# Wide-head attention: values of both examples in one product, weighted values turned by the product itself

## The chip, the cores and the metric

The kernel runs on one core of a Trainium2 chip, as one program. The metric is the device time of one execution in microseconds (us), smaller is better. The engines that matter here are TensorE (PE, matrix products and transposes), VectorE (DVE), ScalarE (ACT) and GpSimd (POOL); each works through its own queue in order, and they wait for each other by semaphores. TensorE reads from SBUF and writes into PSUM, which has eight banks of 512 floats for each of 128 partitions. A product has a stationary operand, loaded first (LDWEIGHTS, shown as PEld), and a moving operand that streams through. All products in this part are in float32, and the profile shows each of them as two MATMUL records; a transpose is one.

## The reference

The whole kernel is a stack of four layers (cross attention, then a feed-forward part) on 32 examples of 64 tokens, 128 wide. The change is in the second layer's attention: 16 heads of 64, queries from the doubly normalised tokens `x`, keys and values from the context, a softmax over 64 context rows for each head, and a gated residual. In short:

```
x1 = layernorm(x);  xn = layernorm(x1) * gamma + beta
q = xn @ w_q;  k, v = split(context @ w_kv)            # 16 heads of 64
p = softmax(q k^T / 8, over the 64 context rows of the example)
x = x + tanh(gate) * ((p v) @ w_out + b_out)
```

## The kernel before, in words

`wide_head_attention` works on 16 tiles. A tile is 128 tokens, two examples of 64, which the code calls b = 0 and 1. The 16 heads are held as eight pairs c, with u = 0 and 1 for the even and the odd head. The work is written as a pipeline of steps by hand (`step(n, p)` for each engine): step n computes the keys of tile n, the queries of tile n-1, the scores and the values of tile n-2, transposes the probabilities and weighs the values of tile n-3, and projects the output of tile n-4. The order of the calls in `step` is the order of each engine's queue, and nothing else sets it. Steps 7 to 14 run in a loop of two steps, the others are unrolled.

TensorE's parts in a step of before, with the lines under which the profile shows them: `scores` (L967, 32 products of 64x64x64, into `pS`), `turn_x` (L941, one transpose), `turn_probs` (L978, eight transposes of `prob` into `pP`), `queries` (L953, eight products of 128x128x128), `turn_out` (L1004, eight transposes of `on` into `pP`), `keys` (L916, as `queries`), `weigh_values` (L993, 32 products of 64x64x64, into `pO`), `project` (L1011, eight products of 128x128x128 that add up in one place of `pP`) and `values` (L931, four products of 128 rows by 64 columns by 512: for each example b and each u).

Queries, keys and values share the two PSUM banks J0 and J1. Each user waits until ScalarE or VectorE has copied out what the user before left there. ScalarE copies `xnT` (L1047), `probT` (L1055), `qT` (L1063), `oT` (L1071) and `kT` (L1079) to SBUF and takes the exponential of `prob` (L1084). VectorE does the two layer norms (L154, L139, L142, L144), the maximum and its subtraction from the scores (L1121, L1123), the sum and its reciprocal (L1133, L1135), the scaling of the weighted values by it (L1140, `on`), the bias and the residual (L1146, L1148) and the copies of the values (L1161). GpSimd copies the context tile (L1094) and takes the powers for the norms (L150).

## Time and profile before

| | us |
|---|---|
| median of 3 runs (1015.64 to 1017.59) | 1017.44 |
| the profiled execution, its own time | 1015.85 |
| its span in the trace | 1014.1 |
| TensorE busy | 787.3 |
| VectorE busy | 625.4 |
| ScalarE busy | 468.8 |
| first product of this attention | 151.4 |
| its last bias add (L1146) | 347.3 |

Times inside the trace count from the start of the span. The profile names an instruction by its engine, its line in the kernel, what it writes and what it reads. "Busy" is the time in which at least one instruction of the engine was in flight; a MATMUL record lasts longer than its share of the array, because successive ones overlap, so the distance from start to start is what a group costs. "issue" is a wait that the profile can't put down to another engine. Names of several buffers are shortened, so `A_v`, `A_on` and `L1w` are tiles of this attention (`L1w` holds its weights).

### The profile page before, as it was taken

What the parts mean: (1) busy time and instruction counts of PE and PEld (TensorE: products, weight loads), DVE (VectorE), ACT (ScalarE), POOL (GpSimd) and SP (SyncE); (2) the same over time, 40 slices, a digit from 0 to 9 for tenths busy, and PEclk for the clock granted to TensorE, in tenths of its full rate; (3) what the DMA queues carried; (4) which work ended last, traced back from release to release, by engine and by line L of the source; (5) the groups of instructions that cost most, each with busy time, mean ns of one, the idle gap of its engine ahead of it and who ended that gap; (6) DMA issues with size and microseconds to landing.
All of it is one profiled execution on the core that took longest, in us unless ns stands there. A gap on an engine that the chain in (4) does not pass through costs nothing.

```text
span 1014.1 us, 24106 instructions
## 1 busy us (share of the span) xinstructions
PE 787.3 (78%) x8041; PEld 650.9 (64%) x8041; DVE 625.4 (62%) x1617; ACT 468.8 (46%) x928; POOL 369.0 (36%) x482
## 2 busy tenths in 40 slices
PE   6998889999999689997377775568777569969005
PEld 3766787888887579996267764467777526643005
DVE  3886766777777677776453333652222388867795
ACT  3886425455544344442144433034454327735753
POOL 5663602111110261101466663125566545550810
PEclk9999699999999979999599999568999769978557
DMA  6300000000000000033323214101111300000001
GB/s 186 96 0 1 1 1 2 3 2 1 0 0 3 1 5 22 21 104 89 103 83 99 72 42 107 41 17 37 43 42 42 90 20 2 0 1 1 0 0 41
DMA packets 49218, 36.06 MB, mean 36 GB/s; under 512 B 7665, under 2 KB 44978, under 8 KB 49138
## 3 DMA queue, kind: packets, MB, share of 16 engines
q1 hardware_dynamic: 43420, 24.45, 8.5%
q0 software_dynamic: 4992, 10.23, 3.7%
q8 instruction: 48, 0.79, 0.3%
q10 hardware_dynamic: 726, 0.33, 0.1%
q14 instruction: 32, 0.26, 0.1%
HBM read 26.73 MB, written 8.26 MB: 35 GB/s over the span
## 4 chain that ended last, share of the span: by engine, by line
PE 67%; DVE 14%; issue 6%; ACT 4%; another core or an unknown queue 3%; DMA 2%; DVEq 2%; POOL 2%; ACTq 1%; SPq 0%; POOLq 0%
PE psum L2057 9%; PE psum L1413 7%; PE psum L2082 4%; PE psum L1011 3%; PE psum L916 3%; PE psum L953 3%; PE psum L931 3%; PE psum L2354 2%; PE psum L308 2%; PE psum L1382 2%; PE psum L1383 2%; PE psum L1384 2%; PE psum L993 2%; PE psum L648 2%
## 5 line engine op out<-in xcount | busy, mean ns | idle before, releaser
L2057 PE MATMUL psum<-E_XT,E_weights 128*128 128x128 f32 x780 | 115.0, 300 | 45.1 <-DVE E_XT L2206 19.1
L2057 PEld LDWEIGHTS psum<-E_XT,E_weights 128*128 128x128 f32 x780 | 103.6, 210 | 54.0 <-DVE E_XT L2206 23.2
L2178 POOL DMA_INDIRECT y_scratch<-E_y,route_place_of x78 | 78.5, 1006 | 74.6 <-DVE E_y L2231 32.0
L2170 POOL DMA_INDIRECT E_rows<-rows_scratch,route_token_of x78 | 77.2, 990 | 58.2 <-DVE route_token_of L1887 29.9
L1670 DVE SCALAR_TENSOR_TENSOR X<-psum,E_gates,X 128x128 f32<-128x128 f32 x256 | 71.8, 345 | 26.2 <-PE psum L1413 25.8
L1413 PEld LDWEIGHTS psum<-E_w,E_h 128*128 128x128 f32 x512 | 67.8, 194 | 11.5 <-ACT E_h L1499 6.0
L2137 ACT ACTIVATE E_h<-psum,cols 128x128 f32<-128x128 f32 x156 | 44.6, 369 | 65.5 <-issue 30.7
L1499 ACT ACTIVATE E_h<-psum,cols 128x512 f32<-128x512 f32 x64 | 43.9, 690 | 61.4 <-PE psum L1384 61.3
L1413 PE MATMUL psum<-E_w,E_h 128*128 128x128 f32 x512 | 68.6, 277 | 4.7 <-ACT E_h L1499 4.0
L2221 DVE TENSOR_TENSOR E_h<-E_sg,psum 128x384 f32<-128x384 f32 x39 | 21.6, 554 | 68.4 <-PE psum L2057 32.0
L203 POOL TENSOR_TENSOR rstd<-vareps,nhalf 128x4 f32<-128x4 f32 x24 | 24.7, 1030 | 104.2 <-DVE vareps L197 104.2
L220 PE MATMUL psum<-ident,xn 128*128 128x128 f32 x80 | 20.2, 402 | 43.0 <-DVE xn L211 33.6
L220 PEld LDWEIGHTS psum<-ident,xn 128*128 128x128 f32 x80 | 13.7, 209 | 50.3 <-issue 25.2
L2082 PE MATMUL psum<-L1w,E_h 128*128 x312 | 43.5, 284 | 0.5 <-DVE E_y L2233 0.5
L150 POOL TENSOR_TENSOR A_A_inner_rstd<-A_A_inner_vareps,nhalf 128x1 f32<-128x1 f32 x16 | 8.8, 551 | 96.0 <-DVE A_A_inner_vareps L144 96.0
L2343 PE MATMUL psum<-ident,Q_amax_rows 128*1 128x128 f32 x5 | 1.8, 352 | 52.4 <-DVE Q_amax_rows L2451 51.7
L2233 DVE TENSOR_TENSOR E_y<-psum,E2b2all 128x128 f32<-128x128 f32 x39 | 11.4, 291 | 50.3 <-PE psum L2082 29.3
L773 POOL TENSOR_TENSOR A_kexp<-E_first,hmask 128x512 f32<-128x512 f32 x32 | 32.7, 1043 | 25.7 <-PE psum L648 25.6
L2082 PEld LDWEIGHTS psum<-L1w,E_h 128*128 128x128 f32 x312 | 39.6, 199 | 1.0 <-issue 0.7
L2053 PE MATMUL psum<-ident,E_rows 128*128 128x128 f32 x78 | 22.8, 292 | 22.3 <-DMA E_rows<-rows_scratch,route_token_of 22.3
L2120 ACT ACTIVATE E_weights<-E_first 128x768 f32 x39 | 33.0, 845 | 14.1 <-issue 13.8
L1047 ACT ACTIVATE A_xnT<-psum,cols 128x128 f32<-128x128 f32 x16 | 7.3, 458 | 64.3 <-PE psum L941 64.3
(342 smaller groups left out, 2164.0 us busy)
## 6 DMA issues: line engine op xcount, KB each, us to landing
routed_back<-y_scratch SPq DMA_DIRECT2D x16, 256.0 KB, 4.8
E_first<-in_L_xattn_W SPq DMA_DIRECT2D x1, 2048.0 KB, 8.6
L1w<-in_L_xattn_W SPq DMA_DIRECT2D x8, 256.0 KB, 4.5
rows_scratch<-xn SPq DMA_DIRECT2D x8, 256.0 KB, 2.3
E_w<-in_L_ffn_routed_w SPq DMA_DIRECT2D x28, 64.0 KB, 1.8
E_raw<-in_L_ffn_w_down SPq DMA_DIRECT2D x8, 176.0 KB
E_rows<-rows_scratch,route_token_of POOLq DMA_INDIRECT x78
y_scratch<-E_y,route_place_of POOLq DMA_INDIRECT x78
```

The source lines that it names most:

```text
L220: tr = pe.transpose(self.bank[:, i * P:(i + 1) * P], self.m.xn[:, g * GT + i, :], self.m.ident[:, :])
L773: ke = pool.tensor_tensor(kexp[:, p, b], kk.broadcast_to([P, HP, S]), m.hmask[:, :].rearrange("p (h o) -> p h o", o=1).broadcast_to([P, HP ...
L916: mm = pe.matmul((J1, J0)[j][:, c * P:(c + 1) * P], w["k"][:, cc * P:(cc + 1) * P], columns(m.ctxT, t, P), start=True, stop=True)
L1413: mm = pe.matmul(y_bank(e, g)[:, i * P:(i + 1) * P], h[:, g % 2, c, i * P:(i + 1) * P], w2[:, p, c, :], start=(c == 0 and i == 0), stop=(c ...
L1499: act.activation(h[:, g % 2, c, :], ring[(C * g + c) % 4], spec["func"], bias=spec["b1"][:, bass.ds(e * C + c, 1)]).then_inc(h_ready.sem, 1)
L1670: st = dve.scalar_tensor_tensor(out=m.X[:, t, :], in0=y_bank(e, g)[:, i * P:(i + 1) * P], scalar=gates[:, t, bass.ds(e, 1)], in1=m.X[:, t, :],
L2057: mm = pe.matmul(out[:, c * P:(c + 1) * P], WE[:, p, (k0 + c) * P:(k0 + c + 1) * P], XT[:, p, :], start=True, stop=True)
L2082: mm = pe.matmul(Y[p][:, 0:P], h[:, p, c, :], W2[:, bass.ds(e, 1), c, :].rearrange("p o d -> p (o d)"), start=c == 0, stop=c == C - 1)
L2120: act.activation(WE[:, i % 2, :], W1[:, bass.ds(e, 1), :].rearrange("p o f -> p (o f)"), ACT.Copy).then_inc(w_ready.sem, 1)
L2137: ac = act.activation(h[:, p, c, :], m.banks[2 + i % 3][:, c * P:(c + 1) * P], spec["func"], bias=spec["b1"][:, bass.ds(e * C + c, 1)])
L2170: pool.indirect_dma_start(out=xg[:, i % 4, :], out_offset=None, in_=rows[:, :], in_offset=bass.IndirectOffsetOnAxis(ap=disp.token_of[:, i: ...
L2178: pool.indirect_dma_start(out=yrows[:, :], in_=y[:, i % 3, :], in_offset=None, out_offset=bass.IndirectOffsetOnAxis(ap=disp.place_of[:, i: ...
```

## The change

The values of a tile are now two products of 128 context rows (both examples) by 128 by 512, one for the even heads into J1, one for the odd heads into J0. VectorE copies the even heads into partitions 0 to 63 of `v`, ScalarE the odd heads into partitions 64 to 127, each in two copies of 64 partitions by 512.

`weigh_values` swaps its operands, so that the result comes out with head dimension by token and needs no transpose: the eight transposes of `turn_out` and the tile `on` are gone. In PSUM, example b now fills bank b of `pO`, and the half of the partitions for head parity u is `x = (u + b) % 2`. So for example 1 the two halves of each pair of heads are swapped; `project` therefore takes a second copy of the output weights with its halves swapped (`L1wo_halves_changed`, two more loads of 256 KB each), and becomes 16 products with 64 columns of the stationary operand instead of eight with 128. The division by the sum of the exponentials, which was in `on`, is now done on `prob` in place, before `turn_probs`, with one VectorE instruction of 128x1024.

The order in a step changes too. On TensorE `project` comes third and `weigh_values` last; on ScalarE the copy of `oT` comes first, straight from `pO`, and the copy of the odd heads' values stands before the exponential; on VectorE the sum, the reciprocal, the scaling of `prob` and the residual come first. Blocks that only moved are left out here.

```diff
-        on = sb("on", [P, 2, H * dh])
-        oT = sb("oT", [P, 2, HP, P])
+        oT = sb("oT", [P, 2, 2, HP, S])
...
-    ov = pO.rearrange("p u (c d) -> p u c d", d=dh)
+    ov = pO.rearrange("p b (c q) -> p b c q", q=S)
...
         def values(t, p):
             pe.wait_ge(*ctx1_ready(t + 1))
             wv = w["v"].rearrange("p (c u d) -> p c u d", u=2, d=dh)
-            for b in range(2):
+            for u in range(2):
                 if before_end(t, 2):
-                    pe.wait_ge(*k_ready(2 * t + b + 5))
+                    pe.wait_ge(*k_ready(2 * t + u + 5))
...
-                for u in range(2):
-                    mm = pe.matmul((J1, J0)[b][u * S:(u + 1) * S, :], ctx1[:, p, b * S:(b + 1) * S], wv[:, :, u, :],
-                                   start=True, stop=True)
-                mm.then_inc(v_ps.sem, 1)
+                pe.matmul((J1, J0)[u], ctx1[:, p, :], wv[:, :, u, :], start=True, stop=True).then_inc(v_ps.sem, 1)
...
         def turn_probs(t, p):
-            pe.wait_ge(*prob_ready(t + 1))
-            if past(t, 2):
-                pe.wait_ge(*tmp_ready(t - 1))
-            elif past(t, 1):
-                pe.wait_ge(*probT_ready(2 * t))
+            pe.wait_ge(*on_ready(t + 1))
+            if past(t, 1):
+                pe.wait_ge(*tmp_ready(t))
...
         def weigh_values(t, p):
             pe.wait_ge(*probT_ready(2 * t + 2))
-            pe.wait_ge(*v_ready(2 * t + 2))
+            pe.wait_ge(*v_ready[0](t + 1))
+            pe.wait_ge(*v_ready[1](t + 1))
             if past(t, 1):
-                pe.wait_ge(*on_ready(t))
+                pe.wait_ge(*oT_ready(2 * t))
             apart(pe, m)
             for c in range(HP):
                 for b in range(2):
                     for u in range(2):
                         rows, toks = slice(u * S, (u + 1) * S), slice(b * S, (b + 1) * S)
-                        mm = pe.matmul(pO[toks, u, c * dh:(c + 1) * dh], probT[rows, p, c, toks], v[rows, p, b, c, :],
+                        x = (u + b) % 2
+                        mm = pe.matmul(ov[x * dh:(x + 1) * dh, b, c, :], v[rows, p, b, c, :], probT[rows, p, c, toks],
                                        start=True, stop=True)
             mm.then_inc(o_ps.sem, 1)
...
         def project(t, p):
             pe.wait_ge(*oT_ready(2 * t + 2))
             for c in range(HP):
-                mm = pe.matmul(pP[:, 0, 0:P], oT[:, p, c, :], w["o"][:, c, :], start=(c == 0), stop=(c == HP - 1))
+                for b in range(2):
+                    mm = pe.matmul(pP[b * S:(b + 1) * S, 0, 0:P], oT[:, p, b, c, :], w["o"][b][:, c, :],
+                                   start=(c == 0), stop=(c == HP - 1))
             mm.then_inc(out_ps.sem, 1)
...
@@ -1039,6 +1025,14 @@
         def step(n, p):
             q = 1 - p
+            if live(n - 4):
+                t = n - 4
+                act.wait_ge(*o_ps(t + 1))
+                if past(t, 2):
+                    act.wait_ge(*out_ps(t - 1))
+                for b in range(2):
+                    act.activation(oT[:, p, b, :, :].rearrange("p c q -> p (c q)"), pO[:, b, :],
+                                   ACT.Copy).then_inc(oT_ready.sem, 1)
...
+            if live(n - 2):
+                t = n - 2
+                act.wait_ge(*v_ps(2 * t + 2))
                 if past(t, 2):
+                    act.wait_ge(*o_ps(t - 1))
+                for b in range(2):
+                    ac = act.activation(v[S:P, p, b, :, :].rearrange("p c d -> p (c d)"), J0[b * S:(b + 1) * S, :], ACT.Copy)
+                ac.then_inc(v_ready[1].sem, 1)
...
@@ -1109,6 +1103,24 @@
         def step(n, p):
             q = 1 - p
+            if live(n - 3):
...
+                dve.tensor_tensor(prob[:, q], prob[:, q],
+                                  rc[:, q, :].rearrange("p (h o) -> p h o", o=1).broadcast_to([P, H, S]),
+                                  ALU.mult).then_inc(on_ready.sem, 1)
...
-                dve.tensor_tensor(by_bank(on[:, q, :].rearrange("p (h d) -> p h d", d=dh)), ov, spread(rc[:, q, :]),
-                                  ALU.mult).then_inc(on_ready.sem, 1)
...
+                dve.wait_ge(*v_ps(2 * t + 1))
                 for b in range(2):
-                    dve.wait_ge(*v_ps(2 * t + b + 1))
-                    dve.tensor_copy(v[:, p, b].rearrange("p c d -> p (c d)"), (J1, J0)[b]).then_inc(v_ready.sem, 1)
+                    cp = dve.tensor_copy(v[0:S, p, b, :, :].rearrange("p c d -> p (c d)"), J1[b * S:(b + 1) * S, :])
+                cp.then_inc(v_ready[0].sem, 1)
...
-        w1["o"] = wide[:, 3, :].rearrange("p (c d) -> p c d", d=D)
-        load(w1["o"], ins["L1_xattn_w_out"].rearrange("(c p) d -> p c d", p=P))
+        w1["o"] = wide[:, 3, :].rearrange("p (c d) -> p c d", d=D), sb("L1wo_halves_changed", [P, HP, D])[:, :, :]
+        load(w1["o"][0], ins["L1_xattn_w_out"].rearrange("(c p) d -> p c d", p=P))
+        for u in range(2):
+            load(w1["o"][1][u * S:(u + 1) * S, :, :],
+                 ins["L1_xattn_w_out"].rearrange("(c v p) d -> v p c d", v=2, p=S)[1 - u])
```

The queue of TensorE in one whole step of the middle, as it stands before (from the projection of one step to the weighing of the next; the first instruction of each part; "L" is its line, "waits" its semaphores):

```order
L1011 MATMUL psum<-L1w,A_oT 128x128 [waits oT_ready]
...
L931 MATMUL psum<-L1w,A_ctx 64x512 [waits k_ready,ctx1_ready]
...
L967 MATMUL psum<-A_kT,A_qT 64x64 [waits sub_ready,q_ready,k_ready]
...
L941 MATMUL psum<-ident,A_xn 128x128 [waits v_ready,xn_ready]
L978 MATMUL psum<-ident,A_prob 128x128 [waits tmp_ready,prob_ready]
...
L953 MATMUL psum<-A_xnT,L1w 128x128 [waits v_ready,xnT_ready]
...
L1004 MATMUL psum<-ident,A_on 128x128 [waits probT_ready,on_ready]
...
L916 MATMUL psum<-ctxT,L1w 128x128 [waits q_ready]
...
L993 MATMUL psum<-A_v,A_probT 64x64 [waits on_ready,probT_ready,v_ready]
```

And the same step in the changed kernel, whose lines are `scores` L964, `turn_x` L938, `project` L998, `queries` L950, `keys` L916, `turn_probs` L973, `values` L930, `weigh_values` L990; as above, the first instruction of each part stands:

```order
L964 MATMUL psum<-A_kT,A_qT 64x64 [waits sub_ready,q_ready,k_ready]
...
L938 MATMUL psum<-ident,A_xn 128x128 [waits v_odd_ready,xn_ready]
L998 MATMUL psum<-L1w,A_oT 64x128 [waits oT_ready]
...
L950 MATMUL psum<-A_xnT,L1w 128x128 [waits v_ready,xnT_ready]
...
L916 MATMUL psum<-ctxT,L1w 128x128 [waits q_ready]
...
L973 MATMUL psum<-ident,A_prob 128x128 [waits tmp_ready,on_ready]
...
L930 MATMUL psum<-L1w,A_ctx 128x512 [waits k_ready,ctx1_ready]
...
L990 MATMUL psum<-A_probT,A_v 64x64 [waits oT_ready,v_odd_ready,probT_ready,v_ready]
```

The transposes of `on` are gone, the projection stands behind the scores and `turn_x`, and between the last product of the values and the projection there are now only `weigh_values`, `scores` and `turn_x`.

ScalarE's queue over the end of one step and the start of the next, before:

```order
L1079 ACTIVATE A_kT<-psum 128x512 [waits k_in_psum]
L1084 ACTIVATE A_prob<-A_prob 128x1024 [waits sub_ready]
L52 UNCONDITIONAL_BRANCH
L52 ISA
L1046 ISA [waits xnT_in_psum]
L1047 ACTIVATE A_xnT<-psum,cols 128x128 [waits q_in_psum]
```

And in the changed kernel, at an unrolled step (L1065 is `probT`, L1073 the odd heads' values, L1078 the exponential, L1034 `oT`, L1041 `xnT`):

```order
L1065 ACTIVATE A_probT<-psum 128x512 [waits probT_in_psum]
L1073 ACTIVATE A_v<-psum 64x512 [waits o_in_psum,v_in_psum]
L1073 ACTIVATE A_v<-psum 64x512
L1078 ACTIVATE A_prob<-A_prob 128x1024 [waits sub_ready]
L1034 ACTIVATE A_oT<-psum 128x512 [waits out_in_psum,o_in_psum]
L1034 ACTIVATE A_oT<-psum 128x512
L1041 ACTIVATE A_xnT<-psum,cols 128x128 [waits q_in_psum,xnT_in_psum]
```

The copies of the odd heads' values, the exponential and the copies of `oT` now follow each other in ScalarE's queue.

## Rows read from the trace of the kernel before

**Rows 1.** Busy time by stretch: two stretches, with granted clock and DMA share last.
```profile
197.30:314.10 116.80, 116.80 (x2011) 98.67 (x2011) 89.02 (x177) 57.68 (x101) 12.88 (x29) 1.00 0.00 1
...
99.90:120.30 20.40, 16.32 (x62) 13.91 (x63) 14.72 (x50) 7.59 (x13) 13.02 (x11) 0.50 0.00 1
```

**Rows 2.** The chain that ended last, one step: start us, us, what.
```profile
219.51 1.09 PE psum L993 x64
220.60 1.98 PE psum L1011 x16
222.58 1.87 PE psum L931 x8
224.45 1.09 PE psum L967 x64
225.54 0.26 PE psum L941
225.80 0.87 PE psum L978 x8
226.67 1.88 PE psum L953 x16
228.55 0.87 PE psum L1004 x8
229.42 1.79 PE psum L916 x16
```

**Rows 3.** Timeline of TensorE: start us, us, line, out<-in, count.
```profile
30.59 1.11 PE L358 MATMUL psum<-A_vbd,A_probT 128*64 128x18 f32 x32
...
222.51 1.94 PE L931 MATMUL psum<-L1w,A_ctx 128*64 128x512 f32 x8
...
225.64 1.04 PE L978 MATMUL psum<-ident,A_prob 128*128 128x128 f32 x8
...
231.14 1.16 PE L993 MATMUL psum<-A_v,A_probT 64*64 64x64 f32 x64
```

**Rows 4.** Timeline of ScalarE in that step.
```profile
226.28 1.08 ACT L1055 ACTIVATE A_probT<-psum 128x512 f32<-128x512 f32 x2
...
231.25 0.60 ACT L1079 ACTIVATE A_kT<-psum 128x512 f32<-128x512 f32 x1 [0.29 <-PE psum L916]
231.74 1.05 ACT L1084 ACTIVATE A_prob<-A_prob 128x1024 f32<-128x1024 f32 x1
```

**Rows 5.** Timeline of VectorE in that step.
```profile
224.50 0.69 DVE L1161 COPY A_v<-psum 128x512 f32<-128x512 f32 x1 [0.17 <-PE psum L931]
...
229.75 1.21 DVE L1133 TENSOR_REDUCE A_sm<-A_prob 128x16 f32<-128x1024 f32 x1
230.99 0.25 DVE L1135 RECIPROCAL A_rc<-A_sm 128x16 f32<-128x16 f32 x1
232.53 1.23 DVE L1140 TENSOR_TENSOR A_on<-psum,A_rc 128x1024 f32<-128x1024 f32 x1 [1.28 <-PE psum L993]
```

**Rows 6.** VectorE by line and form: a product of two SBUF operands, 128x1024.
```profile
L1861 DVE TENSOR_TENSOR route_B<-lane_number,route_lane 128x1024 fp32r<-128x1024 f32 x8 | 9.8, 1221 | 3.9 <-PE psum L1873 3.8
```

**Rows 7.** Timeline of TensorE: the scores of steps 3, 5 and 16.
```profile
168.03 1.16 PE L967 MATMUL psum<-A_kT,A_qT 64*64 64x64 f32 x64
...
189.44 1.16 PE L967 MATMUL psum<-A_kT,A_qT 64*64 64x64 f32 x64
...
317.94 1.16 PE L967 MATMUL psum<-A_kT,A_qT 64*64 64x64 f32 x64
```

**Rows 8.** Timeline of all engines at the attention's end.
```profile
344.10 1.09 ACT L1071 ACTIVATE A_oT<-psum 128x512 f32<-128x512 f32 x2 [3.53 <-PE psum L1004]
...
345.24 2.05 PE L1011 MATMUL psum<-L1w,A_oT 128*128 128x128 f32 x16 [0.80 <-ACT A_oT L1071]
347.32 0.29 DVE L1146 TENSOR_TENSOR A_tmp<-psum,L1bo 128x128 f32<-128x128 f32 x1 [3.51 <-PE psum L1011]
```

**Rows 9.** The page's part 2: DMA engines' busy tenths in 40 slices.
```profile
DMA  6300000000000000033323214101111300000001
```

106 lines of the change are left out of this document (42 added, 64 removed).

## The prediction, written before the changed kernel ran

> **What bounds the kernel now.** I first looked for the stretch of this attention in the busy time by stretch. In its steady middle TensorE is busy for all of 116.8 us at full clock, while VectorE has 89.0 and ScalarE 57.7 us of work [rows 1]. Then the chain that ended last: over a whole step it consists of TensorE alone, nine parts with no wait between them [rows 2]. Their sum is 1.09 + 1.98 + 1.87 + 1.09 + 0.26 + 0.87 + 1.88 + 0.87 + 1.79 = 11.70 us, and the scores of steps 5 and 16 lie 317.94 - 189.44 = 128.50 us apart, 11.68 us a step [rows 7]. So TensorE's work sets the step, and a change pays only if it takes work from TensorE without making it wait. Third, the timelines of ScalarE and VectorE, for the durations that a new wait would be made of [rows 4, 5], and last the end of the attention, where TensorE does wait (0.80 us for `oT`) [rows 8].
>
> **The change part by part.**
>
> *Transposes of `on`.* Eight go, 0.87 us a step [rows 2].
>
> *Values.* Four products with 64 stationary columns become two with 128. Before, eight records of 512 columns take 1.87 us, 0.234 us each; the records of the keys, 128 columns over the full array, take 1.79 / 16 = 0.112 us, so 512 columns one after the other would be 0.448 [rows 2]. The two halves of the array thus already work at the same time. The new form has four records of 0.448 us, 1.79, plus what any part pays on coming from another shape: 1.8 to 1.9 us. I take 1.87, no gain.
>
> *Projection.* 16 products with 64 stationary columns, 32 records. If neighbours (b = 0 and 1, different halves of the array) overlap as the values' halves do, they cost 32 x 0.112 / 2 = 1.79 us, with the margins of the old one 1.98; if not, 3.6. The loads don't bound it: 32 loads of 128x64 with 18 moving columns each take 1.11 us in all [rows 3]. I take 1.98, since the values' row shows this overlap. That these products add up in one place, which the values do not, is left to the rivals.
>
> *Weighing* keeps 32 products of 64x64x64: 1.09 us [rows 2], see the first rival.
>
> *VectorE.* The product on `on`, PSUM to SBUF, 1.23 us [rows 5], becomes one on `prob`, all in SBUF; the like with two SBUF operands takes 1.22 [rows 6]. The two copies of the values keep 512 elements in each partition, so I take 0.69 each as before, on half the partitions. VectorE's work stays at about 9 us of 11.7, and its order leaves slack, worked out below. ScalarE gets two more copies of 512, at 0.49 from start to start [rows 4], about 1 us in 11.7, and it has the room. What counts is where they stand.
>
> *The new wait.* The projection needs `oT` of the tile weighed at the end of the step before. In ScalarE's queue, `oT` stands behind the odd values' two copies and the exponential, and those copies wait for the last product of the values. From the start R of the values:
> - a copy of the values' last product starts 224.50 - 222.51 = 1.99 after R [rows 3, 5];
> - the two copies start 0.49 apart (231.25 to 231.74 [rows 4]), so the exponential starts at R + 2.97;
> - the exponential lasts 1.05 [rows 4] and I take 0.11 of it as overlapped with what follows, as a copy's 0.60 against its pitch of 0.49: `oT` starts at R + 3.91, its second half at 4.40, and ends 0.59 later at R + 4.99;
> - TensorE goes on 0.05 later (345.19 to 345.24 [rows 8]): R + 5.04.
>
> Without that wait TensorE would be there at R + 1.87 + 1.09 + 1.09 + 0.26 = R + 4.31. It stands for 0.73 us, with the queries, keys, transposes and values queued behind. The transposes' 0.87 us are thus given back but for 0.14: the new step is 5.04 + 1.98 (projection) + 1.88 (queries) + 1.79 (keys) + 0.87 (transposes) = 11.56 us. The other waits are met: the queries need `xnT`, which ScalarE makes right after `oT`, 0.46 us beside a projection of 1.98; `turn_probs` stands at R + 10.7 and needs the scaled `prob`. The exponential ends at R + 4.02, the sum, reciprocal and product take 1.24 + 0.30 + 1.23 [rows 5], so R + 6.8. VectorE's next sum starts one step after that, at R + 15.6; I follow its queue (residual at about R + 7.1, norm, maximum, subtraction, second norm, copies of the even values) to an end near R + 14.1. The slack is 1.5 us.
>
> *Filling the pipeline.* From the scores of step 3 to those of step 5 before: 189.44 - 168.03 = 21.41 us [rows 7]. After, counted from the first: `turn_x` waits for the copy of the odd values until 1.25; ScalarE then has an exponential ahead of `xnT`, so the queries start at 2.55, keys 4.43, transposes 6.22, values 7.09, second scores 10.05, projection 12.13, next values 18.65, third scores 21.61. That is 0.2 us longer.
>
> *Emptying it.* Before, from the scores of step 16 to the last bias add: 347.32 - 317.94 = 29.38 us [rows 7, 8]. After, the projection of step 16 starts at 2.08 and that of step 17 at 11.85. The transposes of steps 17 and 18 now wait for the bias add of the step (`pP` is shared), at 14.3 and 22.64, since no keys stand between. Weighing of tile 15 starts at 24.41, a reader of it can start 232.53 - 231.14 = 1.39 later [rows 3, 5] at most, the last projection at 26.89, its bias add 2.08 later at 28.97. That is 0.4 us less.
>
> *Two more loads* of 256 KB: the DMA engines are idle from the third slice of 25 us on [rows 9], and the attention starts at 151 us. Free; what would take the cover away is an attention that starts before 60 us.
>
> *Sum:* +0.2 + 11 x (11.56 - 11.68) - 0.4 = -1.5 us. Against the profiled execution's own 1015.85 (span 1014.1 and 1.75 around it) this gives 1014.35. The runs' median is 1017.44, with the lowest at 1015.64, so the profiled one is among the shorter; I add 0.5 for that and forecast 1014.8. The likeliest case's own range is 1012.5 to 1017. Its width comes from two terms: the chain through ScalarE could be 0.1 us off (1.1 us in 11 steps), and parts that no longer lie between two shapes could be 0.1 us shorter each.
>
> **The rivals.**
>
> *Slower: two products into one bank (0.10).* In `weigh_values` before, the products of u = 0 and 1, which use different rows of the array, write into different banks of `pO`. Now both write into bank b, in different halves of the partitions. No row shows such a pair. If they ran one after the other, the part would take 2.18 instead of 1.09. Its readers could start at 1.87 + 1.09 + 1.39 = R + 4.35 instead of 3.91, so the wait grows by 0.44 and the step becomes 12.00, 0.32 above before: 11 x 0.32 = 3.5. With about 2 x 0.44 + 1.09 more at the end, +0.2 + 3.5 - 0.4 + 2.0 = 5.3: 1021. It decides from a weighing part of about 1.3 us, where the gain of 0.12 is eaten. The Trainium skill (TensorEngine Tiling (Array Packing), Restrictions and Gotchas) says that different row tiles cannot access the same PSUM bank at the same time; whether that holds for different halves of its partitions, no run here shows yet. By that rule the sum would be this rival's, by the rows of the like-shaped part before the forecast's.
>
> *Slower: ScalarE's chain without overlap, or the clock (0.07).* If the five operations take their full durations, 4 x 0.60 + 1.05, the chain is R + 5.49, the step 12.01: about +4, 1019.5. For it speaks that nothing here shows an exponential followed closely by a copy; against it, two copies that take 1.08 together [rows 4]. TensorE's clock could also fall in the new waits: one stretch of 20 us at half clock, with TensorE busy for 16 of it, stands before this attention [rows 1]. But 0.73 us in 11.56 is little, and such a stretch would cost some 8 us.
>
> *Slower: the projection's halves don't overlap (0.03).* Then 3.6 instead of 1.98, 1.6 us in each of 16 steps: +26, 1040.
>
> *Faster: TensorE's parts shrink (0.12).* The old projection takes 1.98 for the records for which the keys need 1.79 [rows 2]; it lies between parts of another shape. If leaving out such neighbours gives back 0.3 us a step outside the wait, it's 11 to 16 times 0.3 more: 1010.5. With no wait at all, the step would be 10.8 and the time 1003; the queue order speaks against it.
>
> *It doesn't do what it says:* TensorE's transposes are gone, but the step is what it was. That is the forecast's other half.
>
> **How the numbers follow.** The forecast's case has 0.68. What a measurement of this kernel can tell from no change is 0.2%, 2 us, and the forecast lies near that border: of its 0.68, 0.35 is faster by more, 0.30 within it, 0.03 slower. With the rivals: faster 0.35 + 0.12 = 0.47, same 0.30 + 0.02 (a weighing only somewhat longer) = 0.32, slower 0.21. The range of 8 in 10 takes in the faster rival and nearly reaches the first slower one: 1010 to 1020.5.
>
> **What would show it.** Steps 11.5 to 11.6 us apart. On TensorE, before the first projection record, a wait of 0.6 to 0.8 us ended by ScalarE's `oT`, eleven or more times; `values` and `project` at 1.8 to 2.0 us; `weigh_values` at 1.1. VectorE waiting 1 to 1.5 us a step for the exponential. Wrong would be: a wait elsewhere, for `prob` or for the even values; a weighing of 2 us; a projection of 3.6; or no wait at the projection.

## The result and the profile after

| | before | after |
|---|---|---|
| median, same chip | 1017.22 us | 1026.28 us |
| ratio after / before, 95% | | 1.0075 [1.0052, 1.0098] |
| ratio, a second time on another chip | | 1.0071 [1.0044, 1.0099] |
| span of the profiled execution | 1014.1 | 1026.7 |
| a second profile of each | 1013.2 | 1023.6 |
| TensorE / VectorE / ScalarE busy | 787.3 / 625.4 / 468.8 | 783.6 / 627.2 / 489.0 |

The forecast was 1014.8 us and slightly faster; the kernel became 0.7% slower, about 7.5 us by the ratio (the two medians differ by 9.1). TensorE has less to do, and still the time grew. Busy time by stretch, the same view and nearly the same stretch as in [rows 1] (columns: stretch, its length, busy time of PE, PEld, DVE, ACT and POOL with the number of instructions, granted clock, DMA share, GB/s):

```profile
197.00:314.00 117.00, 107.69 (x2024) 89.59 (x2018) 87.84 (x178) 69.26 (x118) 13.42 (x30) 1.00 0.00 1
```

TensorE, busy for all of the stretch before, now stands for 9.3 of 117 us, at full clock. The waits of the attention (engine, what it wants, from whom: us in total, times, longest) name the place:

```profile
PE psum L998 <- ACT A_oT L1034: 17.5, 16, 2.4
```

It is the projection, in each of 16 steps, as forecast; but for 1.09 us on average. The chain that ended last (start, us, what), one step of after, to be held against [rows 2], where TensorE alone stood:

```profile
193.05 1.06 ACT A_prob L1078
194.13 1.10 ACT A_oT L1034 x2
195.27 1.97 PE psum L998 x32
197.24 1.98 PE psum L950 x16
199.22 1.91 PE psum L916 x16
201.13 0.87 PE psum L973 x8
202.00 1.73 PE psum L930 x4
203.78 0.57 issue
204.36 0.55 ACT A_v L1073
204.98 1.06 ACT A_prob L1078
206.06 1.10 ACT A_oT L1034 x2
207.20 1.97 PE psum L998 x32
```

From projection to projection it is 207.20 - 195.27 = 11.93 us, where 11.56 was forecast and before had 11.61 to 11.71. The path runs through ScalarE: the copies of the odd values (the 0.57 us called issue are the time of the first one, which starts at 203.76), the exponential, the two copies of `oT`. Its timeline in a step of the loop, with TensorE's values, weighing, scores and first projection record (start, us, engine, line, out<-in, count, idle before and what ended it), answers to [rows 3, 4]:

```profile
225.72 1.88 PE L930 MATMUL psum<-L1w,A_ctx 128*128 128x512 f32 x4
227.53 1.16 PE L990 MATMUL psum<-A_probT,A_v 64*64 64x64 f32 x64
227.64 1.19 ACT L1073 ACTIVATE A_v<-psum 64x512 f32<-64x512 f32 x2 [1.01 <-PE psum L930]
228.58 1.16 PE L964 MATMUL psum<-A_kT,A_qT 64*64 64x64 f32 x64
228.85 1.06 ACT L1078 ACTIVATE A_prob<-A_prob 128x1024 f32<-128x1024 f32 x1
229.94 1.09 ACT L1034 ACTIVATE A_oT<-psum 128x512 f32<-128x512 f32 x2
231.08 0.32 PE L998 MATMUL psum<-L1w,A_oT 128*64 128x128 f32 x1 [1.07 <-ACT A_oT L1034]
```

Read ScalarE's rows by their starts and ends. Two copies in one row last 1.09 when they overlap (`oT`: 2 x 0.60 less 0.11) and 1.19 when they don't (`A_v`). The exponential starts at 228.85, after the copies' end at 228.83; the copies of `oT` start at 229.94, after its end at 229.91. The forecast had an overlap of 0.11 at each of the three borders: copy to copy, copy to exponential, exponential to `oT`.

VectorE's work came out as forecast: the product on `prob` takes 1.22 as in [rows 6], the two copies of the even values 1.37 together, that is 0.69 each, and it waits about 1.5 us a step for the exponential:

```profile
219.54 1.22 DVE L1113 TENSOR_TENSOR A_prob<-A_prob,A_rc 128x1024 f32<-128x1024 f32 x1
227.06 1.37 DVE L1153 COPY A_v<-psum 64x512 f32<-64x512 f32 x2
229.94 1.22 DVE L1109 TENSOR_REDUCE A_sm<-A_prob 128x16 f32<-128x1024 f32 x1 [1.52 <-ACT A_prob L1078]
```

The marks of the attention, the same as in [rows 7, 8]: scores of steps 3, 5 and 16, and the last bias add.

```profile
170.39 1.16 PE L964 MATMUL psum<-A_kT,A_qT 64*64 64x64 f32 x64
...
192.71 1.16 PE L964 MATMUL psum<-A_kT,A_qT 64*64 64x64 f32 x64
...
324.32 1.13 PE L964 MATMUL psum<-A_kT,A_qT 64*64 64x64 f32 x64
...
354.40 0.29 DVE L1120 TENSOR_TENSOR A_tmp<-psum,L1bo 128x128 f32<-128x128 f32 x1 [5.88 <-PE psum L998]
```

| stretch | before | forecast | after | after - before |
|---|---|---|---|---|
| scores 3 to 5 | 21.41 | 21.61 | 22.32 | +0.9 |
| scores 5 to 16, 11 steps | 128.50 | 127.2 | 131.61 | +3.1 |
| scores 16 to last bias add | 29.38 | 28.97 | 30.08 | +0.7 |
| last bias add to the dispatched experts | 150.85 | 150.85 | 152.55 | +1.7 |

The last line takes the start of the stage behind the next one, which shows as the first transpose of `E_rows`, in before and in after:

```profile
498.17 0.45 PE L2053 MATMUL psum<-ident,E_rows 128*128 128x128 f32 x1 [18.22 <-DMA E_rows<-rows_scratch,route_token_of]
```

```profile
506.95 0.45 PE L2046 MATMUL psum<-ident,E_rows 128*128 128x128 f32 x1 [17.91 <-DMA E_rows<-rows_scratch,route_token_of]
```

In the attention 4.7 us were lost, in the untouched feed-forward part behind it 1.7; together 6.4 of the 7.5. A second profile of each kernel gives 4.5 and 2.0. The profiled execution of after has 1.9 us more at the attention's start, where TensorE's granted clock was at its lower level for longer (mean 0.72 against 0.90 over 151 to 168 us; the second profile of after has 0.91 and loses nothing there). What follows 498 and 507 us is 3.8 us longer in after (3.6 in the second pair), in code that is the same; over the other versions that rest lies anywhere from 515 to 526 us, so I put none of it down to the change.

### The profile page after: what moved, and what is told of

Same layout as the page of the kernel before. It is cut to its first block, busy times and chain, and to the rows that moved or that the text cites. A ratio compares the mean times of both kernels' runs of the same rounds, so it can differ in the third digit from the quotient of the medians.

```text
span 1026.7 us, 24239 instructions
## 1 busy us (share of the span) xinstructions
PE 783.6 (76%) x8105; PEld 647.2 (63%) x8105; DVE 627.2 (61%) x1617; ACT 489.0 (48%) x960; POOL 369.1 (36%) x482
## 4 chain that ended last, share of the span: by engine, by line
PE 63%; DVE 12%; ACT 8%; issue 6%; another core or an unknown queue 4%; DMA 2%; POOL 2%; DVEq 2%; ACTq 1%; SPq 0%; POOLq 0%
PE psum L2050 9%; PE psum L1406 7%; PE psum L2075 5%; PE psum L950 3%; PE psum L916 3%; PE psum L998 3%; PE psum L930 3%; PE psum L2347 2%; PE psum L1375 2%; PE psum L1377 2%; PE psum L1376 2%; PE psum L308 2%; PE psum L648 2%; ACT A_oT L1034 2%
## 5 line engine op out<-in xcount | busy, mean ns | idle before, releaser
L2050 PE MATMUL psum<-E_XT,E_weights 128*128 128x128 f32 x780 | 117.9, 305 | 44.0 <-ACT E_XT L2107 18.4
L2050 PEld LDWEIGHTS psum<-E_XT,E_weights 128*128 128x128 f32 x780 | 106.7, 215 | 52.8 <-ACT E_XT L2107 21.4
L998 PE MATMUL psum<-L1w,A_oT 128*64 128x128 f32 x256 | 31.4, 276 | 17.5 <-ACT A_oT L1034 17.5
L1049 ACT ACTIVATE A_qT<-psum 128x512 f32<-128x512 f32 x32 | 19.2, 598 | 46.3 <-PE psum L950 46.3
L998 PEld LDWEIGHTS psum<-L1w,A_oT 128*64 128x64 f32 x256 | 27.5, 137 | 20.4 <-ACT A_oT L1034 20.4
```

The lines of the kernel that those rows point to most:

```text
L998: mm = pe.matmul(pP[b * S:(b + 1) * S, 0, 0:P], oT[:, p, b, c, :], w["o"][b][:, c, :], start=(c == 0), stop=(c == HP - 1))
L2050: mm = pe.matmul(out[:, c * P:(c + 1) * P], WE[:, p, (k0 + c) * P:(k0 + c + 1) * P], XT[:, p, :], start=True, stop=True)
```

## The experiments

All versions start from the changed kernel. "Attention" is the distance from its first product's start to its last projection record's start, "feed-forward" from there to the first transpose of `E_rows`; before has 195.6 and 151.2 (195.7 and 151.0 a second time). Ratios are to before on the same chip.

### Which part costs the time

**exp_late, exp_late2.** The exponential goes behind the copies of `oT` and `xnT` in ScalarE's queue.

```diff
         def step(n, p):                          # ScalarE; behind the copies of oT
+            if live(n - 3):
+                act.wait_ge(*sub_ready(n - 2))
+                pr = prob[:, q].rearrange("p h k -> p (h k)")
+                act.activation(pr, pr, ACT.Exp, scale=scale).then_inc(prob_ready.sem, 1)
...
-            if live(n - 2):
-                act.wait_ge(*sub_ready(n - 1))
-                pr = prob[:, p].rearrange("p h k -> p (h k)")
-                act.activation(pr, pr, ACT.Exp, scale=scale).then_inc(prob_ready.sem, 1)
```

Expected: 

> The changed kernel with one block moved in ScalarE's queue: the exponential of a tile now comes right after the copies of oT in the next step, instead of before them. Theory 1 (the loss is the chain last values product, two copies of odd values, exponential, two copies of oT, projection): the chain in the trace is 1.92 + 1.21 + 1.09 + 1.09 + 0.05 = 5.36 us; without the exponential oT is held only by the weighing and ends near R + 4.3, TensorE's own work gets there at R + 4.3, so the step falls from 11.95 to about 11.0 us and the time from 1026.3 to about 1013.5, below the kernel before (1017.2). Rival A (TensorE's parts themselves, or the two products into one bank, are what costs): the step stays above 11.8, 1024 or more. Rival B (VectorE takes over, since its sum now starts 1.1 us later in the step): a step of about 11.3 and 1017.

> The change with the exponential of a step issued behind the copies of oT and xnT in ScalarE's queue, as exp_late, on another chip beside three others. Theory A (its step is about 11.1 us, so it should be worth what the old values are, and the first ratio, 0.9998, was its chip's): ratio 0.994 to 0.997. Theory B (it has a cost of its own outside the attention): 0.999 to 1.001 again, with the attention near 192 us or less and the feed-forward part above 153.

Measured: 0.9998 [0.9979, 1.0016] and 0.9975 [0.9948, 1.0002]; attention 191.9 and 192.1, feed-forward 154.1 and 153.9. The chain of exp_late2 has a step of 201.41 - 190.57 = 10.84 us, in the loop 11.1:

```profile
190.57 1.97 PE psum L998 x32
...
201.41 1.97 PE psum L998 x32
```

So the step loses 1.09 us, the length of the exponential, when it leaves the chain: the path through ScalarE is shown, and the transposes' 0.87 us come back. The step came out as expected, the time of 1013.5 us did not. The whole gains less than 11 such steps in two places. The transposes at the end wait for the bias add (4.4 us in two waits against 1.0 in after), and TensorE's clock falls 8 us before the attention's end, beside a feed-forward part that is 2.9 us longer. By stages -3.6 + 2.9 = -0.7 us, 0.9993, which lies between the two ratios. The stages speak for theory B of exp_late2 (a cost of its own outside the step); its ratio, just outside both forecasts, doesn't decide.

**old_values, old_values2.** The values again as four products of 64 stationary columns with one example's rows each, copied by VectorE alone as 128x512; the rest as in the change.

```diff
-            for u in range(2):
+            for b in range(2):
...
-                pe.matmul((J1, J0)[u], ctx1[:, p, :], wv[:, :, u, :], start=True, stop=True).then_inc(v_ps.sem, 1)
+                for u in range(2):
+                    mm = pe.matmul((J1, J0)[b][u * S:(u + 1) * S, :], ctx1[:, p, b * S:(b + 1) * S], wv[:, :, u, :],
+                                   start=True, stop=True)
+                mm.then_inc(v_ps.sem, 1)
...
-                for b in range(2):
-                    ac = act.activation(v[S:P, p, b, :, :].rearrange("p c d -> p (c d)"), J0[b * S:(b + 1) * S, :], ACT.Copy)
-                ac.then_inc(v_ready[1].sem, 1)
```

Expected: 

> The changed kernel with one part undone: the values as before (four products of 64 columns by example, both copied by VectorE with 128 partitions); ScalarE copies no values, so its exponential starts right after the keys' copies. Theory 1: oT waits only for the weighing, the projection stands still for less than 0.2 us, step about 10.9 to 11.0, time about 1013. Rival A: 1024 or more. Rival B (VectorE bound): step about 11.3, 1017.

> The values go back to four products of 64 stationary columns, copied by VectorE alone, and everything else is as in the change; this time it runs on one chip with the version that has the projection ahead of the transpose of xn (swap2). Theory A (ScalarE's chain of copies and exponential cost the change its gain, and without the values' copies in it TensorE never waits for oT): step near 10.9 to 11.2 us, ratio to before again 0.990 to 0.995, 1008 to 1012 on a chip where before takes 1017. Theory B (the gain of the first run was the chip's): ratio 0.998 to 1.002. Against swap2: if TensorE's own work is the bound in both, the two lie within 0.2% of each other.

Measured: 0.9922 [0.9894, 0.9950] and 0.9955 [0.9927, 0.9983]; attention 190.3 and 188.9, feed-forward 153.7 and 153.0. In old_values2 TensorE has the chain to itself again:

```profile
191.71 1.96 PE psum L999 x32
...
198.43 1.87 PE psum L930 x8
200.30 1.09 PE psum L991 x64
201.39 0.95 PE psum L966 x62
202.34 0.26 PE psum L940
202.60 1.96 PE psum L999 x32
```

The step is 202.60 - 191.71 = 10.89 us, less than before by about 0.8. The turned weighing and the removed transposes are worth 0.5 to 0.8% of the time by the ratios, and 0.3 to 0.5% by the stages (-5.3 + 2.6 and -6.8 + 1.9 us); the new form of the values, which saves TensorE 1.87 - 1.73 = 0.14 us a step, takes all of that and more away by putting its copies into ScalarE's chain. Of the two ratios the first is below and the second just above what was expected of it.

**one_load.** The second copy of the output weights isn't loaded; both halves of `project` read the first. It leaves out the swapped halves, so the output of example 1 isn't the reference's.

```diff
-        w1["o"] = wide[:, 3, :].rearrange("p (c d) -> p c d", d=D), sb("L1wo_halves_changed", [P, HP, D])[:, :, :]
+        w1["o"] = (wide[:, 3, :].rearrange("p (c d) -> p c d", d=D),) * 2
```

Expected: 

> The changed kernel without the two added loads; the projection of example 1 uses the first copy of the output weights, so the second copy's swapped halves are left out. It asks where the part of the loss outside this attention comes from (the profiled run is 12.6 us longer, the attention itself 6.7). If the two loads disturb the first layer (its end is 1.7 us later in the trace): about 1024.5, with the first layer ending near 100 us. If that was scatter between executions: 1026.3 as the changed kernel.

Measured: 1.0060 [1.0036, 1.0085], attention 202.0. The interval overlaps that of the change, and the attention starts at 150.6 us, in the change's two profiles at 151.9 and 151.1: the loads cost nothing that shows.

### Why ScalarE's chain is longer than forecast

**full.** ScalarE copies all 128 partitions of the bank into a tile of its own, from whose upper half the weighing reads. Same number of instructions, same 512 columns, same place in the queue. It leaves the odd heads' values of example 0 wrong.

```diff
-                    ac = act.activation(v[S:P, p, b, :, :].rearrange("p c d -> p (c d)"), J0[b * S:(b + 1) * S, :], ACT.Copy)
+                    ac = act.activation(v2[:, p, b, :, :].rearrange("p c d -> p (c d)"), J0[:, :], ACT.Copy)
```

Expected: 

> The changed kernel with ScalarE's two copies of the odd values over all 128 partitions of the bank, without a shift of partitions, into a tile of their own (so the copy for example 0 keeps the rows where they are: the values of example 0's odd heads are left wrong). In the changed kernel two such copies of 64 partitions take 1.21 us from the first's start to the exponential and the exponential 1.09 to oT; copies of 128 partitions start 0.49 apart. If copies of 64 partitions are what doesn't overlap: the exponential starts 0.98 after the first copy, the step falls by 0.2 to 0.35 us and the time by 2.5 to 4 us, to about 1023. If the number of partitions doesn't matter: no change, 1026.

Measured: 0.9988 [0.9959, 1.0017]; attention 195.9, feed-forward 153.2. Its timeline of ScalarE in an unrolled step:

```profile
201.42 1.08 ACT L1074 ACTIVATE A_v<-psum 128x512 f32<-128x512 f32 x2 [1.01 <-PE psum L931]
202.39 1.06 ACT L1079 ACTIVATE A_prob<-A_prob 128x1024 f32<-128x1024 f32 x1
203.34 1.09 ACT L1035 ACTIVATE A_oT<-psum 128x512 f32<-128x512 f32 x2
```

Copies to exponential 0.97, exponential to `oT` 0.95: the overlaps of the forecast (0.98 and 0.94) are there, and the step is 204.48 - 192.94 = 11.54 us by its chain, where the forecast had 11.56. The step's error is thus wholly in these three borders: they lose their overlap with the copies of 64 partitions and have it with copies of 128. The step fell by 0.39 us, a little more than expected. The ratio lies 3.5 us below what the stages give (+0.2 and +2.1 us), so the reading rests on the step and not on the ratio. The edit changes two things, the number of partitions and the tile; the next two runs keep the tile.

**noshift.** Both copies read and write partitions 64 to 127, to see whether it is the shift from the lower half to the upper. Example 0's odd heads get example 1's rows.

```diff
-                    ac = act.activation(v[S:P, p, b, :, :].rearrange("p c d -> p (c d)"), J0[b * S:(b + 1) * S, :], ACT.Copy)
+                    ac = act.activation(v[S:P, p, b, :, :].rearrange("p c d -> p (c d)"), J0[S:P, :], ACT.Copy)
```

Expected: 

> The changed kernel with both of ScalarE's copies of the odd values reading partitions 64 to 127 and writing the same ones (so example 0 gets example 1's rows). If the shift of partitions (reading 0 to 63, writing 64 to 127) is what keeps the first copy from overlapping with the second: they start 0.49 apart, the step falls 0.12 us, the attention 1.5 us. If the number of partitions is: 0.60 apart, attention 202 as in the changed kernel.

**even_by_act.** ScalarE writes its bank into partitions 0 to 63, VectorE the other into 64 to 127. The weighted values are those of swapped heads.

```diff
-                    ac = act.activation(v[S:P, p, b, :, :].rearrange("p c d -> p (c d)"), J0[b * S:(b + 1) * S, :], ACT.Copy)
+                    ac = act.activation(v[0:S, p, b, :, :].rearrange("p c d -> p (c d)"), J0[b * S:(b + 1) * S, :], ACT.Copy)
```

Expected: 

> ScalarE copies its bank of values into partitions 0 to 63 and VectorE the other bank into 64 to 127, still 64 partitions each; the weighted values are therefore those of swapped heads. What is read is the distance of ScalarE's successive instructions. Theory A (an instruction of 64 partitions that doesn't touch both halves in the same way, or simply any of 64 partitions, ends ScalarE's overlap): the copies start 0.60 apart, the exponential 0.60 after the second, and oT 1.09 after the exponential starts, as in the change. Theory B (only upper partitions, 64 to 127, as the target lose it): copies 0.49 to 0.50 apart and oT 0.95 after the exponential. Since in the change both copies write 64 to 127, and one of them reads 0 to 63, a third outcome is possible: copy to copy 0.60 apart where the halves differ, 0.49 where they are the same.

Measured, one execution each: 1028.06 and 1027.43 us, attention 203.0 and 202.8. First noshift, then even_by_act:

```profile
226.96 1.08 ACT L1073 ACTIVATE A_v<-psum 64x512 f32<-64x512 f32 x2 [1.02 <-PE psum L930]
228.06 1.06 ACT L1078 ACTIVATE A_prob<-A_prob 128x1024 f32<-128x1024 f32 x1
229.14 1.08 ACT L1034 ACTIVATE A_oT<-psum 128x512 f32<-128x512 f32 x2
```

```profile
226.70 1.20 ACT L1073 ACTIVATE A_v<-psum 64x512 f32<-64x512 f32 x2 [1.02 <-PE psum L930]
227.80 1.04 ACT L1078 ACTIVATE A_prob<-A_prob 128x1024 f32<-128x1024 f32 x1
228.87 1.09 ACT L1034 ACTIVATE A_oT<-psum 128x512 f32<-128x512 f32 x2
```

| border | change | noshift | even_by_act | full |
|---|---|---|---|---|
| copy to copy | no overlap | overlap | no overlap | overlap |
| copy to exponential | no overlap | no overlap | overlap | overlap |
| exponential to `oT` | no overlap | no overlap | no overlap | overlap |

In each of the two one of three overlaps comes back: noshift's two copies last 1.08 together, and even_by_act's exponential starts 1.10 after the copies' row, before that row's end. Their steps are 11.8 instead of 11.93, as one overlap of 0.11 says. Their attentions aren't shorter all the same, for another reason: from the scores of step 16 to the last bias add noshift takes 355.25 - 322.67 = 32.58 us against 30.08 in the change, with a mean granted clock of 0.62 over 344 to 348.5 us and 0.57 over 351 to 355, where the change has full clock; even_by_act shows the same. None of the theories on record fits all of it: "any instruction of 64 partitions" fails on noshift's copies and even_by_act's exponential, "only upper partitions" on even_by_act's other two borders. The one case on record that fits even_by_act's copies and noshift's is the third, that copies overlap where they use the same halves and not where the halves differ. That it depends on which halves the neighbours use is shown for the copies. That it isn't the tile is shown for the first two borders, each of which comes back in one of these runs with the tile kept. Why the exponential, itself of 128 partitions, isn't overlapped with `oT` in any version but full stays open. The trace of exp_late2 narrows it: there the exponential (201.24, 1.06 long) stands behind the copies of `oT`, and ScalarE's copy of `xnT` starts at 202.19, 0.11 before its end. So an exponential can overlap with a copy behind it in a kernel that has the copies of 64, where they don't stand right ahead of it.

### The time behind the attention

**before_again, after_again.** Both kernels once more without an edit, to see what repeats.

Expected: 

> The kernel before, traced a second time. The attention's length should repeat at 195.6 us; the stages behind it show how much they scatter by themselves. In all traces of the changed kernel's variants the feed-forward stage right behind the attention took 153 to 154 us, before 151.2. If that belongs to the change, it is 151 again here; if it is scatter, 151 to 154.

> The changed kernel once more, on the chip on which the next variant runs. The attention's length from its first product to its last (202.2 us in the first trace, 195.6 before) should repeat within 0.5 us if it is set by the queues. The rest of the kernel was 6 us longer in that trace; if that comes from the change, the rest repeats too and the ratio to before is 1.0075 again; if it is scatter between executions, the ratio lies nearer 1.0065, which is what the attention's 6.6 us make.

Measured: after_again 1.0071 [1.0044, 1.0099]; attention 200.2 against 195.7, feed-forward 153.1 against 151.0. Both differences repeat. The granted clock shows the second. Windows behind the attention in before (it ends at 347), then in after (it ends at 354); columns as above, the clock is the third number from the end:

```profile
356.00:369.00 13.00, 12.06 (x49) 10.76 (x48) 7.71 (x12) 6.01 (x8) 10.81 (x10) 0.50 0.00 1
370.00:376.00 6.00, 2.95 (x20) 2.33 (x19) 5.16 (x18) 3.16 (x5) 2.18 (x4) 1.00 0.00 0
376.00:382.00 6.00, 6.00 (x45) 5.53 (x44) 5.18 (x21) 2.75 (x4) 0.76 (x2) 1.00 0.09 25
```

```profile
359.00:364.00 5.00, 3.73 (x19) 3.38 (x18) 4.56 (x13) 2.17 (x4) 4.79 (x6) 0.50 0.00 0
364.00:378.00 14.00, 13.06 (x53) 11.66 (x53) 8.77 (x15) 6.01 (x8) 11.58 (x12) 0.50 0.00 1
379.00:382.00 3.00, 0.86 (x6) 0.44 (x5) 2.26 (x9) 2.89 (x5) 0.66 (x2) 1.00 0.00 0
382.00:385.00 3.00, 3.00 (x15) 2.71 (x14) 3.00 (x12) 0.66 (x2) 0.00 (x0) 0.55 0.02 5
```

Behind both, TensorE runs at 1.2 instead of 2.4 GHz. In before that lasts 17.1 us, beginning 5.4 us after the last projection record; in after it begins 4.4 us after it (4.1 the second time), lasts 20.5 us and comes back for another 3.4.

**warm_tail, warm_tail2, exp_warm, swap_warm.** Does TensorE's idle time at the end of the attention make that stretch longer? 16 extra transposes, read by nobody, fill part of its waits in each of two steps; in the change (the edit shown), in exp_late and in swap (below).

```diff
+            if isinstance(n, int) and n in (NT + 2, NT + 3):
+                pe.wait_ge(*v_ready[0](NT))
+                pe.wait_ge(*v_ready[1](NT))
+                for i in range(16):
+                    pe.transpose(J0[:, 0:P], m.ident[:, :], m.ident[:, :])
             if live(n - 4):
                 project(n - 4, p)
```

Expected: 

> As the change, with 16 extra transposes of the identity (128x128, into J0, read by nobody) ahead of the projection in the last two steps but one of the attention (n = 18 and 19), where TensorE would stand and wait. Theory A (TensorE's idle time at the end of the attention is what lengthens the stretch of low clock in the feed-forward part that follows, 20.5 us and 3.4 more instead of 17.1 before): the low stretch goes back to about 17 us, and the feed-forward part to 151 us from 153; the attention itself 0 to 1.5 us longer. Theory B (the low stretch is set by what comes after, not by these waits): low stretch 20 to 24 us and 153 us, as in the change. Time about 1026 to 1028 by B, 1024 to 1026 by A.

> The change with the same extra transposes, timed. Its single profile had a feed-forward part of 151.3 us against 152.9 in the change, and an attention of 204.1 against 202.2. If the clock explains the 2 us outside the attention: feed-forward part 151 to 151.5 again, ratio 1.004 to 1.007 (the change 1.0071 to 1.0075). If the first look was chance: feed-forward part 153, ratio 1.007 to 1.009.

> As exp_late2, with 16 extra transposes ahead of the projection in each of the two steps n = 18 and 19. If TensorE's idle time at the attention's end sets the length of the low clock behind it: feed-forward part 151 to 152 us instead of 153 to 154, and the ratio 0.002 below exp_late2's, less what the extra work adds to the attention (0 to 1.5 us). If not: the same low stretch, and the ratio equal or up to 0.0015 above.

> The version called swap and swap2 (the change with the old values, and with turn_x ahead of the scores), plus the same 16 extra transposes ahead of the projection in steps n = 18 and 19. If the low clock's length follows TensorE's idle time: feed-forward part 151 us instead of 153, ratio 0.994 to 0.995 (swap had 0.9955 and 0.9963). If not: 0.996 to 0.998.

| | attention | low clock begins after it, lasts | feed-forward | ratio |
|---|---|---|---|---|
| warm_tail | 204.1 | 5.6, 17.1 us | 151.3 | one execution, 1025.77 us |
| warm_tail2 | 202.6 | 3.7, 20.5 + 3.4 | 153.4 | 1.0064 [1.0039, 1.0089] |
| exp_warm | 194.8 | 4.3, 20.5 + 3.4 | 153.0 | 0.9968 [0.9935, 1.0002] |
| swap_warm | 190.6 | 5.6, 17.1 | 151.2 | 0.9935 [0.9905, 0.9965] |

warm_tail over one window, where the clock is low throughout, and then back for good; and warm_tail2, the same kernel, where it falls a second time:

```profile
360.00:377.00 17.00, 15.45 (x63) 14.09 (x64) 11.62 (x23) 7.55 (x11) 14.76 (x16) 0.50 0.00 1
378.00:388.00 10.00, 7.05 (x47) 6.12 (x46) 8.84 (x33) 5.21 (x8) 2.34 (x5) 1.00 0.04 13
```

```profile
358.00:378.00 20.00, 17.63 (x72) 15.89 (x73) 14.29 (x34) 8.17 (x12) 16.78 (x17) 0.50 0.00 1
378.00:381.00 3.00, 1.08 (x6) 0.59 (x4) 2.34 (x9) 2.13 (x4) 1.51 (x3) 0.98 0.00 0
381.00:385.00 4.00, 3.50 (x13) 3.21 (x14) 3.86 (x15) 1.06 (x3) 0.00 (x0) 0.57 0.00 0
```

The filling helped in two profiles of four, and the same kernel did both. In the ten us ahead of the last projection record TensorE is busy for 7.8 us in before, 5.9 in after and 8.5 in both warm_tail and warm_tail2, and of these two one has the long stretch and one the short. So the cause on record, idle time at the end, isn't shown. What holds over all 18 profiles is the link between the numbers: four have a feed-forward part of 151.0 to 151.3, and in these four the clock falls 5.4 to 5.6 us after the attention; in the other 14 it falls earlier and the part takes 152.8 to 154.1. The 2 us thus go with the clock in every profile, though no run set the clock by itself; what decides when it falls stays open, and swap_warm's ratio doesn't stand clear of swap's.

### The best version

**swap, swap2.** The old values as in old_values, and `turn_x` ahead of the scores. The expectation recorded for swap2 tells this edit wrongly ("as the change", "behind the projection"), and so does the one for old_values2, which speaks of it; both runs were of this one.

```diff
+            if live(n - 1):
+                turn_x(n - 1, q)
             if live(n - 2):
                 scores(n - 2, p)
-            if live(n - 1):
-                turn_x(n - 1, q)
```

Expected: 

> The variant with the values and their copies as before (which ran 0.8% shorter than the kernel before), with turn_x ahead of the scores on TensorE. In that variant's loop TensorE stands 0.38 us at a step's start, between two parts of 1.1 us (issue, at the loop's branch). If it is the loop's instructions that a short part ahead can't cover, turn_x before the scores changes little (0.1 us in every second step, under 1 us in all): ratio 0.992. If the scores wait for something else there (the subtraction, the copies of q and k), the wait moves or goes: up to 0.38 in every second step, 2 us: 0.990.

> As the change, but turn_x stands behind the projection on TensorE. The first run gave 0.9955 [0.9928, 0.9982] and an attention of 187.6 us. Theory A (the wait for oT is what is to be shortened, and xnT is no longer behind it in ScalarE's queue): step 11.0 to 11.5, ratio 0.993 to 0.998. Theory B (the first run's gain was chance of the chip): ratio 1.000 to 1.007, that is the change's.

Measured: 0.9955 [0.9928, 0.9982] and 0.9963 [0.9937, 0.9989], 1011.07 and 1011.60 us; attention 187.6 and 187.2, feed-forward 152.8 and 153.0. It beats before and the change, but both ratios expected of swap, 0.992 and 0.990, were missed, and against old_values2 on one chip (1010.45) there is no difference: in the loop the steps are 11.45 and 11.0 us in turn, there 11.5 and 10.95. Moving `turn_x` brings nothing that shows. With swap_warm (1012.51 on a third chip) the best interval is 0.9905 to 0.9965. The gain of the turned weighing, with the values left alone, is about 0.5%.

## Why the prediction was wrong

*TensorE's parts: right.* Projection 1.97 (forecast 1.98), queries 1.98 (1.88), keys 1.91 (1.79), transposes 0.87 (0.87), values 1.73 (1.87). The halves of the projection overlap: its records for b = 0 and 1 start 0.01 us apart and the pairs every 0.11. The five lengths are those in the chain. By the timelines, in which the values start 0.16 us before their place in the chain (201.84 and 202.00), the sum behind the wait is 11.93 - 5.36 = 6.57 us, 0.05 above the forecast's 6.52.

*The place of the wait: right.* It stands before the projection, on `oT`, 16 times. Nothing else waits in the middle, and VectorE has its slack.

*The failed step: "the new wait", its terms from the copies to `oT`.* The path was right; the forecast put it at 5.04 us, and it measured 5.36. By the same timelines, from the start of the values:

| term | forecast | after | full |
|---|---|---|---|
| values' start to the first copy | 1.99 | 1.92 | 1.92 |
| first copy to exponential | 0.98 | 1.21 | 0.97 |
| exponential to `oT` | 0.94 | 1.09 | 0.95 |
| the two copies of `oT` | 1.08 | 1.09 | 1.09 |
| to the projection | 0.05 | 0.05 | 0.05 |
| sum | 5.04 | 5.36 | 4.98 |

The Trainium skill (ScalarE: Activation LUTs, What ACT_TABLE_LOAD costs) states that back-to-back ACTIVATEs overlap, by about 93 ns. The copies of 128 partitions agree (two in 1.08 to 1.09 us, each 0.60, so 0.11); the copies of 64 in the change don't (1.19), and for these the measurement decides.

The prediction carried the overlap of two copies of 128 partitions [rows 4] over to copies of 64 and to their borders with the exponential. That was worth 0.23 + 0.15 us a step, and the step's margin to before was 0.12. It turns 11 x (-0.12) = -1.3 us into +3.1, since the loop adds a little (12.0 and 11.95 in turn from projection to projection, 11.96 on average). The prediction had this as a rival, "ScalarE's chain without overlap": step 12.01, about 1019.5 us, chance 0.07. Its step was right to 0.05. It was given little for two copies that overlap, although the prediction says itself that no row showed a copy close behind an exponential. By that lack the two ends, 5.04 and 5.49, stood on an equal footing, one on each side of no change.

*Filling and emptying: too small.* +0.9 instead of +0.2 and +0.7 instead of -0.4. Each of these stretches holds two or three of the same chains: the two steps of the first took 10.39 and 11.93 us where the forecast had 10.05 and 11.56. At the end the wait reaches 2.4 us.

*The rest of the time: missed.* The forecast took it as unchanged. The longer stretch of low clock behind the attention, and 1.7 to 3.0 us more in the feed-forward part, are in every version of the change without extra transposes, whatever its attention takes. With these 2 us the stages of the second pair of profiles give 4.5 + 2.0 = 6.5 us or 1.0064, inside both intervals.

*The rivals.* Two products into one bank is refuted: the weighing takes 1.09 us for 64 records (200.30 to 201.39 in the rows of old_values2; in the change's timeline 227.53 to 228.58 = 1.05). The Trainium skill (TensorEngine Tiling (Array Packing), Restrictions and Gotchas) says that different row tiles cannot access one PSUM bank at the same time; here u = 0 and 1 use different rows and write into different halves of the partitions of one bank, at no cost, so for that case the measurement decides against it. Halves of the projection that don't overlap would have needed 3.6 us. Parts that shrink: the values did (0.14), but queries and keys grew by 0.22, so TensorE's parts together got no shorter.

*The range* ended at 1020.5, below the 1026.28 measured. It took in the rival's step but not its share at both ends, nor anything outside the attention.

## What to carry to other kernels

Where an edit takes work from the bounding engine and puts a chain through another engine in its way, compare the chain, end to end, with what the bounding engine has left to do meanwhile; a margin of 0.1 us a step isn't a gain until each border of the chain has been seen in a row of the same shape. Time each half of a double change alone: here one half was worth +0.5% and the other cost over 1%. Look into the untouched stage behind the change too, since its clock can start in another state.

## What the runs showed of the hardware

- In before and in full, where all of ScalarE's instructions here cover 128 partitions, one starts about 0.11 us before the one ahead has ended. With copies of 64 partitions in the chain this can be lost: two copies of 64x512 took 1.19 to 1.20 instead of 1.08, and an exponential started 0.02 us behind its neighbour instead of 0.11 before its end. So did the copy of 128 partitions behind that exponential (0.03 behind it). Two 64-partition copies from and into the same half did overlap (1.08).
- Products that use different halves of the array's rows and write into different halves of the partitions of one PSUM bank ran at the same time: 64 records of 64x64 in 1.05 to 1.09 us.
- Accumulating products of 64 stationary columns in the two halves of one bank overlap fully: 32 records in 1.97 us, as 16 records of 128 columns take 1.98.
- A stage that nobody touched took 151.0 to 151.3 us with one stretch at 1.2 GHz near its start (17.1 us), and 152.8 to 154.1 us with a longer one and a second behind it (20.5 and 3.4 us; in exp_late and exp_late2 27.3, begun 8 us ahead of the stage, and 6.8).
